# Cross-attention and feed-forward layer on one core: row scores in four PSUM banks, low parts of the normed x on GpSimd, block 14's out-product in the body of block 15

## What is computed

```
x = x + xattn(layernorm(x), ctx);  x = x + ffn(layernorm(x))
xattn: w = softmax(q1 k1^T) - lam * softmax(q2 k2^T); attn = w v
       attn * rsqrt(mean(attn^2) + eps) * g * (1 - lambda0) @ Wo^T
ffn:   h = gelu((layernorm(x) g1 + b1ln) @ ternary(w1)^T + b1)
       out = (layernorm(h) g2 + b2ln) @ ternary(w2)^T + b2
```

## Time and profile before

| | us |
|---|---|
| median of three runs (2376.98 to 2382.32) | 2377.75 |
| the profiled execution | 2379.91 |
| its span, first to last instruction | 2377.8 |
| TensorE busy | 2266.3 |
| VectorE busy | 1693.5 |
| ScalarE busy | 1381.4 |
| GpSimd busy | 1020.0 |

### The profile page before, as it was taken

The page is one execution under the profiler, slowest core; times in us unless marked ns, Lnnn a source line. Parts: engine busy times, 40 slices in busy tenths (PEclk is TensorE's granted clock), DMA queues, the critical chain, the costliest instruction groups (busy, mean ns, idle before and its releaser), DMA issues.

```text
span 2377.8 us, 35354 instructions
## 1 busy us (share of the span) xinstructions
PE 2266.3 (95%) x13567; PEld 1058.6 (45%) x13567; DVE 1693.5 (71%) x2659; ACT 1381.4 (58%) x2001; POOL 1020.0 (43%) x807
## 2 busy tenths in 40 slices
PE   8679999999999999999999999999999999999978
PEld 5344534444353444435344444535444453544433
DVE  4667858687685868678686867868576786857673
ACT  3335666566575656657565655656555565655544
POOL 0101625437172543617163462816346281634517
PEclk9779999999999999999999999999999999999999
DMA  7312203131220303122140312213041221302000
GB/s 264 104 45 63 45 24 89 29 83 44 75 52 24 94 24 87 39 67 45 33 104 20 94 33 67 46 51 74 18 106 33 67 46 47 79 20 72 15 23 18
DMA packets 164796, 140.54 MB, mean 59 GB/s; under 512 B 81648, under 2 KB 133420, under 8 KB 164116
## 3 DMA queue, kind: packets, MB, share of 16 engines
q1 hardware_dynamic: 164628, 138.28, 22.2%
HBM read 51.80 MB, written 20.36 MB: 30 GB/s over the span
## 4 chain that ended last, share of the span: by engine, by line
PE 69%; DVE 19%; ACT 4%; SPq 3%; issue 2%; DMA 2%; POOL 1%; POOLq 0%; ACTq 0%; DVEq 0%
PE ps L1471 12%; PE ps L1483 9%; PE ps L1493 6%; PE ps L1321 6%; PE ps L1322 5%; PE ps L1323 5%; DVE arena L1010 5%; PE ps L1416 5%; PE ps L1394 4%; PE ps L1423 4%; DVE arena L1109 4%; PE ps L1369 3%; DVE arena L1003 3%; DVE attn_raw L1048 2%; SPq L470 2%
## 5 line engine op out<-in xcount | busy, mean ns | idle before, releaser
L590 POOL TENSOR_TENSOR attn_raw<-attn_raw 128x512 f32<-128x512 f32 x448 | 612.7, 1387 | 109.6 <-ACT attn_raw L747 102.2
L1471 PE MATMUL ps<-rows,w1T 128*128 128x512 f16 x2048 | 485.4, 380 | 6.6 <-DVE rows L1104 6.6
L1010 DVE TENSOR_REDUCE arena<-ps 128x3 f32<-128x462 f32 (+1 forms) x704 | 412.4, 617 | 89.7 <-PE ps L1369 88.7
L556 POOL TENSOR_TENSOR q<-q 128x512 f16<-128x512 f32 x128 | 151.4, 1188 | 685.0 <-ACT q L693 683.9
L742 ACT ACTIVATE attn_raw<-ps,vec_cols,wstep 128x512 f32<-128x512 f32 x256 | 198.4, 775 | 203.0 <-PE ps L1471 200.4
L1109 DVE SCALAR_TENSOR_TENSOR arena<-attn_raw,vec_cols,arena 128x512 f16<-128x512 f32 x256 | 231.2, 903 | 73.4 <-ACT arena L745 71.6
L1471 PEld LDWEIGHTS ps<-rows,w1T 128*128 128x128 f16 x2048 | 192.5, 98 | 198.2 <-DVE rows L1104 10.2
L1493 PE MATMUL ps<-w2T,arena 128*128 128x512 f16 x1088 | 271.2, 379 | 0.0
L713 ACT ACTIVATE arena<-ps 128x1024 f32<-128x1024 f32 x128 | 131.6, 1028 | 228.4 <-PE ps L1394 228.4
L1030 DVE SCALAR_TENSOR_TENSOR p<-arena,p 128x512 f16<-128x512 f32 x128 | 88.2, 689 | 236.6 <-ACT p L717 236.6
L1369 PE MATMUL ps<-k_att,stack_raw 96*128 96x154 f16 x2048 | 223.0, 234 | 31.8 <-DVE arena L1010 27.4
(11 more groups left out here) (187 smaller groups left out, 3466.9 us busy)
## 6 DMA issues: line engine op xcount, KB each, us to landing
stack_raw<-q SPq DMA_DIRECT2D x768, 64.0 KB, 2.0
arena<-in_x SPq DMA_DIRECT2D x64, 256.0 KB, 2.7
out<-arena SPq DMA_DIRECT2D x64, 256.0 KB, 2.0
arena<-in_x SPq DMA_DIRECT2D x15, 1024.0 KB, 6.9
arena<-in_L_ffn_w SPq DMA_DIRECT2D x7, 1024.0 KB, 10.0
stack_raw<-in_L_xattn_Wq SPq DMA_DIRECT2D x8, 256.0 KB, 5.7
k_att<-k_store SPq DMA_DIRECT2D x4, 490.0 KB
k_store<-attn_raw SPq DMA_DIRECT2D x12, 160.0 KB
```

The source lines that it names most:

```text
L590: ins = pool.tensor_tensor(acc[:, e, :], acc[:, e, :], src[:, j % NG, :], ALU.add)
L1010: dve.tensor_reduce(negmax[:, tt, u0:u1], ps[:, row_bank(c, tb), 0:(u1 - u0) * S].rearrange("p (u s) -> p u s", s=S), AX.X, ALU.max, negat ...
L1471: ins = pe.matmul(ps[:, B_H + j % 2, :], w1T[:, k, j * P:(j + 1) * P], rows16[:, e, k, :], start=(k == 0 and e == 0), stop=(k == KD - 1 an ...
```

## The change

- Row scores rotate over banks 6, 7, 0 and 1 for blocks from 2 on (blocks 0 and 1 keep two). Tile tb then waits for the maxima of tile tb-4, and tile 2 for the last query's copy.
- x_rows_lo moves from VectorE to GpSimd, behind sum_gelu(j) of j = 7 to 10.
- In iteration 14 the body has no ffn_step. All four row tiles of block 14's out-product are made in iteration 15: tile 0 in the front, tile 1 around s0, half of tile 2 after v1, the rest of tile 2 and tile 3 around the out-projection and the transposes. VectorE adds tiles 2 and 3 after h_lo. Iteration 15 has its own order, LAST.
- Block 15's rows are loaded into xrows16, free by then, ahead of block 14's stores; its transposes and hidden products use banks 4, 6, 0 and 1.
- In the last body GpSimd adds the constants at j = 3, 6, 9 and 12, and gelu_sums stand before the last ffn_step.

The diff, cut to its core (x_res is residual(c) throughout: x_last for block 15, else x_res):

```diff
+LAST = [(w[0], int(w[1:] or 0)) for w in (
+    "e0 g f0 h1 y0 s0 i1 s1 v0 y1 z0 s2 v1 h2 s3 v2 z1 s4 a0 v3 s5 v4 s6 a1 v5 s7 v6 a2 v7 a3").split()]
+CONST_AT = {3: 0, 6: 1, 9: 2, 12: 3}
...
         def row_bank(c, tb):
-            return B_O + tb % 2
+            return (B_O, B_L, 0, 1)[tb % row_banks(c)]
+        def row_banks(c):
+            return 2 if c < 2 else 4
+        def ffn_bank(c, tt):
+            if c == NBLK - 2:
+                return (2, B_Q, B_Q, B_L)[tt]
...
+        def h_bank(c, k):
+            return (B_H, B_O, 0, 1)[k] if c == NBLK - 1 else B_H + k
+        def attend(i):
+            return LAST if i == NBLK - 1 else ATTEND if i else FIRST
...
             def load_x_res(c, tt):
-                if c:
+                if c == NBLK - 1:
+                    wait(sp, s_q, c, QM, QM)
+                elif c:
                     wait(sp, s_stored[tt], c, 16, 0)
...
             def iteration(i):
-                if i:
+                if i == NBLK - 1:
+                    for tt in range(TT):
+                        load_x_res(i, tt)
+                    for tt in range(TT):
+                        store(i - 1, tt)
+                elif i:
...
+            def x_rows_lo(c, tts):
+                for tt in tts:
+                    wait(pool, s_xr_hi, c - 2, TT, tt + 1)
+                    pool.tensor_tensor(x_split(tt)[:, 1, :], x_in[:, tt, :], x_split(tt)[:, 0, :],
+                                      ALU.subtract).then_inc(s_xr_lo, 1)
...
                 for j in range(JH):
                     if j:
                         sum_gelu(i, j)
+                    if ahead2 and j in X_LO_AT:
+                        x_rows_lo(i + 2, X_LO_AT[j])
+                    if i == NBLK - 1 and j in CONST_AT:
+                        add_constant(i, (CONST_AT[j],))
...
-            add_constant(NBLK - 1, range(TT))
             power(3, s_gln, s_rstd4, NBLK - 1)
...
                 h_lo(i)
                 if ahead2:
                     ln1_offsets(i + 2)
+                if not ahead:
+                    for tt in (2, 3):
+                        add_ffn(i - 1, tt, ffn_bank(i - 1, tt))
+                    for tt in (2, 3):
+                        add_shift(i - 1, tt)
...
-                    if ahead2 and j in X_LO_AT:
-                        x_rows_lo(i + 2, X_LO_AT[j])
...
-                if tb >= 2:
-                    wait(pe, s_tmax, c, NT, tb - 1)
+                if tb >= row_banks(c):
+                    wait(pe, s_tmax, c, NT, tb - row_banks(c) + 1)
+                elif tb == 2:
+                    wait(pe, s_q32, c, QM, QM)
...
                         wait(pe, s_gln, c - 1, 1, 1)
-                        wait(pe, s_y, c - 1, TT, 2)
+                        wait(pe, s_y, c - 1, TT, 1 if c == NBLK - 1 else 2)
...
                     out_projection(i, tt, (0, 1, 2))
+                if not ahead:
+                    ffn_late(i - 1, 2, range(JH // 2, 3 * JH // 4))
                 out_projection(i, 0, (3,))
                 out_projection(i, 1, (3,))
                 rms_sums(i)
                 out_projection(i, 2, (3,))
                 out_projection(i, 3, (3,))
+                if not ahead:
+                    ffn_late(i - 1, 2, range(3 * JH // 4, JH))
+                    ffn_late(i - 1, 3, range(3 * JH // 4))
...
                 h_transposes(i)
+                if not ahead:
+                    ffn_late(i - 1, 3, range(3 * JH // 4, JH))
...
-                banks = (2, 3) if ahead else range(TT)
+                banks = () if i == NBLK - 2 else (2, 3) if ahead else range(TT)
...
                 for j in range(JH - FLAG, JH):
-                    ffn_step(i, j, banks)
+                    if not ahead and j == JH - 1:
+                        gelu_sums(i)
+                    if banks:
+                        ffn_step(i, j, banks)
...
-            gelu_sums(NBLK - 1)
```

More of the change, by code:

```diff
@@ L225, in build, with residual @@
         x_res = x_res_raw.rearrange("p (s d) -> p s d", s=TT)
+        x_last = xrows16[:].rearrange("p e k t -> p (e k t)").bitcast(F32).rearrange("p (s d) -> p s d", s=TT)
+        def residual(c):
+            return x_last if c == NBLK - 1 else x_res
         signs_late = x_res_raw.bitcast(F16).rearrange("p (n e t) -> p n e t", n=4, e=2)
@@ L594, in iteration @@
                 ahead, ahead2 = i < NBLK - 1, i < NBLK - 2
-                for what, n in ATTEND if i else FIRST:
+                for what, n in attend(i):
                     if what == "g" and i:
@@ L731, in h_hi @@
                 for k in range(KD):
[L732 removed]
+                    act.activation(rows16[:, 0, k, :], ps[:, h_bank(c, k), :], ACT.Identity,
                                    scale=g1_col[:, k:k + 1]).then_inc(s_ht_hi, 1)
@@ L998, in x_lo @@
                                       xrows16[:, 0, :, cols], ALU.subtract).then_inc(s_xt_lo, 1)
[L1000 to L1004, removed]
             def row_max(c, tb):
@@ L1163, in iteration @@
                     elif what == "y" and i:
-                        add_ffn(i - 1, n, ffn_bank(n))
+                        add_ffn(i - 1, n, ffn_bank(i - 1, n))
                     elif what == "z" and i:
@@ L1455, in h_transposes @@
                     wait(pe, s_q32, c + 1, QM, 5)
-                else:
-                    wait(pe, s_y, c - 1, TT, TT)
                 for tt in range(TT):
@@ L1477, in ffn_late @@
                 for j in js:
-                    if j == 0 and tt == 2:
+                    if c == NBLK - 2:
+                        if tt == 0:
+                            wait(pe, s_gg_lo, c, JH, j + 1)
+                        elif j == 0 and tt == 1:
+                            wait(pe, s_gelu, c, JH, JH)
+                        elif j == 0 and tt == 2:
+                            wait(pe, s_y, c, TT, 2)
+                        elif j == 0:
+                            wait(pe, s_ol2, c + 1, KD, KD)
+                    elif j == 0 and tt == 2:
                         wait(pe, s_gelu, c, JH, JH)
@@ L1560, in iteration @@
                         row_scores(i + 1, tb)
-                    if j >= FLAG:
+                    if j >= FLAG and banks:
                         ffn_step(i, j - FLAG, banks)
```

29 lines of the change are left out of this document (14 added, 15 removed).

## The result

The changed kernel takes 2403.43 us (median of 2396.51, 2403.43 and 2405.37), before 2377.75: ratio 1.0096, 95% interval 1.0059 to 1.0133: slower by 1.0%, clear of noise. The profiled execution took 2403.43 us, its span 2401.3. The page's line that answers to the earlier trace rows: TensorE is busier by 23 us, with the same matmuls.

A forecast was written before the change was run, and what follows sets the result against it. GpSimd's chain and TensorE were taken as level before the scores, with GpSimd saturated after the change. Terms 0.9 + 3.9 + 0 + 1.6 - 1.7 - 0.5 - 0.3 = +3.9 us gave 2381.6 us median; own range 2373 to 2386, 8-in-10 range 2369 to 2394.

The forecast's parts named there:

- the clock: TensorE's new waits before sums and scores, blocks 1 to 13: rival that its clock falls, +8 us, 2390, chance 0.10.
- the lag: GpSimd's sum_gelu(15) in blocks 1 to 13 ends at 53.7 against 53.4 us: +0.3 us a block, +3.9 in all.
- half clock at the sums: Sign in the profile, at the sums of gelu, that the forecast sum was too low; no size given.
- Block 14: From hidden(0) to the next scores: no change, ends -1 and +1.5; clock falling in a 5 us gap, +1.6 us.
- Block 0: Keeps two banks; low parts on GpSimd lengthen the steps at j = 7 to 10: +0.9 us, ends 0 and 2.
- Attention, out-projection and norm of block 15: Reordered matmuls fill TensorE's waits: -1.7 us in the attention, -0.5 in out-projection and second norm.
- Tail: After the last body: sums of gelu before the last out-product step, GpSimd's constants inside the body, -0.3 us.
- The first rival: At j = 7 to 10: a low part costs GpSimd more than 1.23 us; at 1.4, 2392 us; chance 0.30.
- x: GpSimd's added time per low part at j = 7 to 10: taken as 1.2 us, between 1.02 and 1.7.
- The last rival: Faster, GpSimd isn't the bound: 2371 us, or 2353 if its lag didn't count; chance 0.17 for both, 0.05 for the second.

The follow-up runs named there:

- the last two runs: On the kernel with h1 ahead of the maxima: two of GpSimd's four constants moved behind the power, 2352.77 us; then those two also behind VectorE's scale and shift, 2339.76 us.

## Why the prediction was wrong

**The step that failed is the clock.** The forecast, 2381.6 us, had the mechanism of the lag right and its size too: sum_gelu(15) at 53.7 (measured 53.9), TensorE's wait before the sums 1.3 to 1.8 us (1.7; it came there at 52.2 us for 52.5), about 1 us before the scores (0.75), +0.3 us a block (+0.24). That the clock would fall in that wait was put at nothing in the sum and stood there as a rival, with a chance of 0.10 and 0.6 us a block; "half clock at the sums" was among its signs of a sum too low. It fell in 11 of 13 blocks, and cost 0.8 us where it was down for 3.4 us and 2.4 where it was down for 6.8: 20 us instead of 8. Filling the gap with eight matmuls took the time to 2380.5, where the forecast without a clock had put it.

Two readings led there. The forecast compared the coming wait with gaps of 1.70 and 1.94 us that had left the clock alone, each seen once, and one of 2.23 us that hadn't, and took the length of idle time for all that counts. The same trace speaks against such a line: a second gap of 2.23 us, before hidden(0) of block 15 (2309.03 in the earlier trace rows), left the clock at 1.0, as this window shows.

```profile
2309.10:2313.00 3.90, 3.90 (x19) 1.68 (x20) 1.63 (x3) 2.14 (x5) 0.00 (x0) 1.00 0.02 4
```

And the gap of 1.70 us came before a fall in the run with low parts on GpSimd alone. The forecast's gaps also stood between matmuls of 512 columns; the new one stands right before 1.8 us of one-column matmuls, and there the clock fell behind 0.48 us of waiting in 11 blocks of 13. No run holds all else fixed and changes only those neighbours, so what share is theirs stays open. And it priced a fall by the shortest in the trace, 3 us, though the one in block 15 had lasted 6.8; the slack of 1 us swallows half of a short fall and little of a long one.

**Block 14**: 0 + 1.6 was forecast for it up to the scores, +3.6 measured. The body is as forecast (sums at 49.7 for 50.0, the wait of 4.6 us there for 5), but the clock was at half for 10.2 us. The windows, the second row from the gap's end:

```profile
2244.57:2249.18 4.61, 0.01 (x1) 0.00 (x1) 4.42 (x6) 0.70 (x2) 4.47 (x5) 0.81 0.01 2
2249.20:2257.50 8.30, 8.30 (x31) 5.38 (x32) 1.91 (x7) 0.00 (x0) 5.73 (x5) 0.50 0.44 134
```

**The other terms.** Block 0: +0.9 forecast, +1.7 measured. Attention, out-projection and norm of block 15: -2.2 forecast, -3.0 measured. Tail: -0.3 forecast, +0.2 measured, as the sums start at 55.6 for 55.3; GpSimd with its constants is late there.

**The first rival**, low parts over 1.23 us each, didn't decide: by the forecast's sum x is (53.87 - 48.9) / 4 = 1.24, and GpSimd's rows give 1.2. But the run with two on each engine ends 2.0 us after that with none and only 0.5 before that with four, so the agreement of 53.7 holds for four only. **The last rival**, GpSimd not being the bound, falls with its lag seen in every block.

What the forecast missed on the way: two of the three parts of the change are worth -28 us (four banks) and +35 us (low parts on GpSimd) alone, and +53 together with the banks already there. It called the gain of the banks "worth something only if sum_gelu(15) ends earlier too", and it does, by 2.1 us, as long as GpSimd isn't given more.

## What to carry to other kernels

Before work is moved to an engine at 43%, read that engine's queue in the stretch where the work lands: here it had 0.65 us of idle time in a step, and lost them as soon as TensorE stopped stalling. A wait that a change creates on TensorE is to be priced with the clock's fall behind it, above all beside matmuls of few columns, and the first thing to try on it is to fill it, if need be with work that nobody reads. Not to make the wait is better still where it can be had: with the low parts left on VectorE the kernel was 30 us faster than with the filler.

## What the runs showed of the hardware

- One-column matmuls keep TensorE "busy" in the profile, but behind a wait as short as 0.48 us right before them its clock fell to half in 11 of 13 blocks, and with no wait before them behind none of 13 (the kernel before). Half clock lasted 3.4, 6.8 or 10.2 us here.
- The same wait of 1.70 us, with the same matmuls on both sides, left the clock at 1.0 in one kernel and came before 0.50 in another; 2.48 us came before a fall in 7 of 13 blocks.
- The Trainium skill (TensorE: Matmul & The Clock Gate, Part 1) says that the throttled state is the default and that activity releases it. The filler's run agrees: with eight matmuls in the wait the clock stayed at 1.0 in all of blocks 1 to 13.
- A VectorE operation on four numbers in each partition takes 1.2 us when GpSimd runs 128x512 operations beside it, and 0.2 us when GpSimd is made to wait (scale and shift in the last two runs).
- gelu_lo and GpSimd's sums draw each other out: over its 256 executions gelu_lo's mean is 903 ns before and 1240 ns in the changed kernel, whose GpSimd never rests there.
